# A fourth input slot, a bank reader moved to ScalarE, and a changed order on VectorE in a convolution kernel

## The chip, the cores and the metric

The kernel runs on one core of a Trainium2 chip. The metric is the device time of one execution in microseconds (us). The five engines of the core (TensorE or PE, VectorE or DVE, ScalarE or ACT, GpSimd or POOL, SyncE or SP) each run a program of their own in order and meet at semaphores. Transfers are issued on SyncE's queue and run on 16 DMA engines.

## The reference

The input x has 8 images of 64 channels and 224 x 224 pixels. It is group-normalised in 32 groups. The result is x plus two terms: a 3 x 3 convolution of the normalised x with its bias (`res`), and a map that comes from the first image alone (wavelet filters, an attention on each group of channels, another 3 x 3 convolution and a leaky ReLU) and is added to every image:

```python
x = x + _L0_conv_ref(_gn(x), ...)
# in _L0_conv_ref:
res = conv3x3(x, W_id, b_id)
cA, cH, cV, cD = _swt2_level3(x[0])
...
out = jax.nn.leaky_relu(conv3x3(dmt, W_enc, b_enc), 0.01)
return out + res
```

## The kernel before

The kernel has three stages: what comes before the maps, the maps of the first image (`encoder`), and the convolution of the eight images (`main`), which is the stage of the change. It begins near 800 us and fills the rest of the time. The map of the encoder stays in on-chip memory (`e_map`) and is added by seeding the PSUM banks with it.

**Bands.** The two halves of an image's rows lie on the lower and the upper 64 partitions. Each half has 14 bands of 8 rows, with two rows more for the neighbours, so a band is 128 x 2240 values of float32. Weights and data are split into a high and a low part in float16, and three products of the parts (high-high, low-high, high-low) are accumulated. Seven bands of an image are *direct*: three rows of weights for each output row, into `g_bank[0]` (PSUM banks 0 and 1) and `g_bank[1]` (banks 2 and 3). Seven are *minimal*: they form differences of rows (in place, rows 0 to 7 of the band) and sums of rows (`sums`), and need four products `m0` to `m3` in `a_bank` (banks 4, 5) and `b_bank` (banks 6, 7) instead of six.

**Rounds.** The stage has 56 rounds. In round q TensorE works on the direct band q+1 and the minimal band q, in turn: `first_direct` (72 matmuls), `product_m2` (36), `middle_direct` (72), `product_m1` (36), `last_direct` (72), `product_m0` (36), `product_m3` (36). All matmuls have line L1766, and a round has 360. `product_m1` overwrites what `double` reads, so it waits for `double`. `product_m0` waits for `seed_odd`.

**VectorE's round** is written out by hand: `odd_rows(q-1)` (L1969, two instructions, waits for `m3` of round q-1, which is the end of that round on TensorE), `diffs_low(q)` (L1946), `neighbour_sums(q+1)` (L1928, L1929), a part of the next image's weights in two of the seven rounds of an image (`build_part`, L1734 to L1745), `read_direct(q+1, 0)` (L1954), `split(q+2)` (L1619), `seed_odd(q)` (L1961), `differences(q+1)` (L1935), `sums_low(q+1)` (L1940), `read_direct(q+1, 1)` (L1954).

**ScalarE's round**: `diffs_high(q)` (L1863), `high(q+2)` (L1606), `double(q)` (L1879, writes `twice` = -2 times `a_bank` plus a mean), `full(q+2)` (L1612), `seed_direct(q+2, 0)` (L1633), `sums_high(q+1)` (L1871), `even_rows(q)` (L1886, waits for `m0`), `seed_minimal(q+1)` (L1893), `seed_direct(q+2, 1)` (L1633).

**Results.** `stage[0]` holds the results of a direct band and `stage[1]` those of a minimal band, each 128 x 1792; in `stage[1]` the left half of each group of 448 columns holds even rows and the right half odd rows. `stored[0]` and `stored[1]` count the stores that have landed, four of 224 KB for a band, 16 counts each.

**SyncE's round** q: wait for both readers of the direct band q, four stores (L1833); wait for the even and the odd rows of band q-1, four stores (L1833); two loads of x of two transfers each (L1584). A load into a slot waits until the band that lay there has been split into its parts (`split_done`).

**Memory.** There are XS = 3 slots for bands of x. The six sets of weights in float32 (`base`, three loaded, three made by GpSimd in `sets`) and `twice` lie behind the first two slots, `made` holds a half of the six sets while it is built.

Of the kernel before, what the change touches and what calls it, by code (L numbers as in the profile page):

```python
# [18 lines left out]
P = 128  # L19
# [8 lines left out]
RH = R + 2  # L28
NT = 2 * W
XS = 3  # L30
# [51 lines left out]
Ahead = namedtuple("Ahead", "load weights_load dummies pads norms spread build normed high full split edges root partners sets spread_rows clear first_seed conv_first conv_rest")  # L82
# [831 lines left out]
def encoder(nc, x, t, scratch, rows_last, rows_out, step_in, ps, psum, sb, sem, top, weff, u32, b32, bn, b16, shift, inside, e_max, einv, b_id, early, e_map,  # L914
# [5 lines left out]
    with ExitStack() as s4:  # L920
# [72 lines left out]
        def sync(sp):  # L993
# [45 lines left out]
            ahead.load(sp, 2)  # L1039

# [310 lines left out]
        def gpsimd(pool):  # L1351
# [89 lines left out]
            both_rows(NE - 1)  # L1441

# [3 lines left out]
def main(nc, x, t, out, ps, psum, sb, sem, top, pool_of, early, e_map, partner, mv_all, norm_all, w_max, unit):  # L1446
# [3 lines left out]
    with ExitStack() as s5:  # L1450
        tail = sb(s5, "tail", [P, RH * W + 4 * NT * 2 + V_N + SET_N + TMP_N])
# [23 lines left out]
        assert 2 * RH * W + SET_N + 4 * W <= D_EVEN_AT  # L1475
        x_hi = [f16_rows(pooled(AT_HI0, HI_N), RH), f16_rows(pooled(AT_HI0 + 2 * HI_N, HI_N), RH)]
        x_lo = [f16_rows(pooled(AT_HI0 + HI_N, HI_N), RH), f16_rows(early[:, RH * W:RH * W + HI_N], RH)]
        sums = pooled(AT_S, 2 * CH * W)
        first_made = sums[:, 0:TMP_N].rearrange("p (s k e) -> p s k e", s=NSET // 2, k=3)
# [3 lines left out]
        diag = early[0:C, RH * W:RH * W + B * C].rearrange("p (i e) -> p i e", i=B)  # L1483
# [5 lines left out]
        made = carve(TMP_N).rearrange("p (s k e) -> p s k e", s=NSET // 2, k=3)  # L1489
# [35 lines left out]
        g_read = sem(top, "g_read")  # L1525
# [18 lines left out]
        built = sem(top, "built")  # L1544
# [45 lines left out]
        def weights_load(sp):  # L1590
            for s in range(2):
                sp.dma_start(base[C * s:C * s + C, 0:3, :, :].rearrange("p s k e -> p (s k) e"), t["w_id"]).then_inc(weights_in, 16)
            sp.dma_start(ident, t["ident"]).then_inc(weights_in, 16)
# [34 lines left out]
        def seed_direct(act, j, g):  # L1628

            i, b = direct(j)  # L1630
            if j:
                act.wait_ge(g_read, 2 * j - 1 + g)
            act.activation(g_bank[g], e_rows[:, :, b, g, :, :].rearrange("p r q w -> p r (q w)"), ACT.Identity,  # L1633
                           scale=lane(r_out, i), bias=lane(mean_r, i)).then_inc(g_seeded, 1)
# [72 lines left out]
        def sets(pool):  # L1707
# [7 lines left out]
            def of(s):  # L1715
                return base[:, s, :, :].rearrange("p k e -> p (k e)")
# [8 lines left out]

        def build_part(dve, i, h):

            n = 10 * i + 1 + 5 * h
            v = made if i else first_made
            flat = v.rearrange("p s k e -> p (s k) e")  # L1730
            if i == 0 and h == 0:
                dve.wait_ge(sets_made, 6)
            dve.wait_ge(building, n)
            dve.tensor_tensor(flat, base[:, 3 * h:3 * h + 3, :, :].rearrange("p s k e -> p (s k) e"),  # L1734
# [93 lines left out]
        def sync(sp):  # L1828
# [16 lines left out]
            load(sp, 3)  # L1845
            load(sp, 4)
            for q in range(NW):
                store_direct(q)
                if q:
                    store_minimal(q - 1)  # L1850
                load(sp, 2 * q + 5)
                load(sp, 2 * q + 6)
# [4 lines left out]
        def scalar(act):  # L1857
# [39 lines left out]
            for q in range(-1, NW):  # L1897
# [14 lines left out]
                if q + 1 < NW:  # L1912
                    seed_minimal(q + 1)
                if q + 2 < ND:
                    seed_direct(act, q + 2, 1)

        def vector(dve):
            def neighbour_sums(j):

                i, b = minimal(j)  # L1920
                k = place_w(j)
                landed(dve, k)
# [26 lines left out]
            def read_direct(j, g):  # L1949
# [3 lines left out]
                dve.wait_ge(g_done, 2 * j + g + 1)  # L1953
                dve.tensor_scalar(stage[0][:, :, g, :], g_bank[g], lane(m_out, i), None, ALU.mult).then_inc(g_read, 1)  # L1954

            def seed_odd(j):
# [4 lines left out]
                dve.tensor_tensor(b_bank, a_bank, twice, ALU.add).then_inc(b_seeded, 1)  # L1961
# [11 lines left out]
            for q in range(-1, NW):  # L1973
                if q > 0:
                    odd_rows(q - 1)
                if q >= 0:
                    diffs_low(q)
                if q + 1 < NW:
                    neighbour_sums(q + 1)
                i, b = direct(q + 1) if q + 1 < ND else (B, 0)  # L1980
                if i + 1 < B and b in DIRECT[2:4]:
                    build_part(dve, i + 1, DIRECT.index(b) - 2)
                if q + 1 < ND:
                    read_direct(q + 1, 0)
# [7 lines left out]
                if q + 1 < ND:  # L1992
                    read_direct(q + 1, 1)
# [17 lines left out]
        def gpsimd(pool):  # L2011
# [14 lines left out]
            for i in range(B):  # L2026
                if i + 1 < B:
# [5 lines left out]
                      sets=sets, spread_rows=spread_rows, clear=clear, first_seed=first_seed, conv_first=conv_first, conv_rest=conv_rest)  # L2033
# [43 lines left out]
```

## Time and profile before

| | |
|---|---|
| runs of the kernel | 1819.07 us median of 3 (1810.22 to 1823.49) |
| the profiled execution | 1814.87 us, of which the span of its instructions is 1813.1 us |
| granted TensorE clock, mean of the span | 0.994 |
| TensorE matmuls busy | 1761.4 us (97%) |
| VectorE busy | 1450.2 us (80%) |
| ScalarE busy | 1238.6 us (68%) |
| GpSimd busy | 545.5 us (30%) |
| stores of results | 448 of 224 KB, median 3.6 us from issue to landing |

Busy times are shares of the whole span, so they average over the three stages. Matmuls overlap one another, and a busy TensorE need not be at its peak rate; the number of matmuls that start in a stretch tells its rate. The granted clock is 1.00 at the upper of the two levels of TensorE's clock (2.4 GHz) and 0.50 at the lower (1.2 GHz).

### The profile page before, as it was taken

To read this page: it belongs to the slowest core of one execution; us is meant where nothing else is said; L and a number is where in the kernel's file an instruction comes from. 1 tells how busy PE (TensorE), PEld (TensorE's weight loads), DVE (VectorE), ACT (ScalarE), POOL (GpSimd) and SP (SyncE) were. 2 spreads that over 40 slices of the span, in tenths; PEclk is the share of its full clock that TensorE was granted. 3 is DMA by queue.
4 is the path that set the end of the run, shared out by engine and by line. 5 is a ranking of instruction groups with operands and counts; after the bars stand their busy time and mean duration, and the time that the engine had idled before them with its cause. 6 is when DMAs were issued, how large, how long until landed. Compare 5 with 4: busy or idle time off the path is not lost. (4 is left out here: it accounts for less than half of the span.)

```text
span 1813.1 us, 69228 instructions
## 1 busy us (share of the span) xinstructions
PE 1761.4 (97%) x31540; PEld 1470.2 (81%) x31540; DVE 1450.2 (80%) x1926; ACT 1238.6 (68%) x1339; POOL 545.5 (30%) x365
## 2 busy tenths in 40 slices
PE   9999999999999999989999999999999999999997
PEld 9997999999999999965577797767966756967676
DVE  5665578778777887668989889888889888888886
ACT  5555666666666666667776777767776767766774
POOL 0005788888888888640000000000000000000000
PEclk9999999999999999999999999999999999999999
DMA  8884399888888888458998998998989989989994
GB/s 186 245 296 126 122 274 227 212 219 216 212 215 215 215 215 206 100 125 204 235 234 223 239 239 226 240 240 229 238 224 236 247 213 232 242 219 230 249 234 140
DMA packets 132964, 391.84 MB, mean 216 GB/s; under 512 B 49884, under 2 KB 50656, under 8 KB 118464
## 3 DMA queue, kind: packets, MB, share of 16 engines
q1 hardware_dynamic: 132672, 387.43, 82.7%
q8 instruction: 247, 4.05, 1.0%
q14 instruction: 45, 0.37, 0.1%
HBM read 258.88 MB, written 128.45 MB: 214 GB/s over the span
## 5 line engine op out<-in xcount | busy, mean ns | idle before, releaser
L1766 PE MATMUL ps<-big,tail 64*64 64x448 f16 x3840 | 323.3, 353 | 11.8 <-DVE ps L1961 7.8
L1766 PE MATMUL ps<-pool_of 64*64 64x448 f16 x5184 | 302.5, 352 | 7.9 <-DVE pool_of L1625 4.2
L1766 PE MATMUL ps<-pool_of,tail 64*64 64x448 f16 x4896 | 300.1, 349 | 0.7 <-issue 0.7
L1766 PE MATMUL ps<-big,pool_of 64*64 64x448 f16 x3552 | 278.5, 352 | 17.1 <-DVE ps L1961 11.9
L1292 DVE BATCH_NORM_STATS2 pool_of<-big 128x6 f32<-128x448 f32 x392 | 232.2, 616 | 76.4 <-DMA big<-in_x 76.3
L1766 PEld LDWEIGHTS ps<-pool_of 64*64 64x64 f16 x5184 | 196.2, 107 | 68.0 <-issue 10.1
L1766 PEld LDWEIGHTS ps<-pool_of,tail 64*64 64x64 f16 x4896 | 189.6, 106 | 59.3 <-issue 1.3
L1066 PE MATMUL ps<-pool_of 112*128 112x246 f16 x1344 | 218.8, 271 | 1.7 <-DVE pool_of L1280 0.8
L1070 PE MATMUL ps<-pool_of 112*128 112x168 f16 x1344 | 217.8, 243 | 0.0
L1766 PEld LDWEIGHTS ps<-big,tail 64*64 64x64 f16 x3840 | 169.0, 107 | 57.9 <-DVE ps L1961 10.4
L1069 PE MATMUL ps<-pool_of 112*128 112x90 f16 x1344 | 201.3, 206 | 0.0
L1766 PEld LDWEIGHTS ps<-big,pool_of 64*64 64x64 f16 x3552 | 134.3, 107 | 69.8 <-DVE ps L1961 15.8
L1886 ACT ACTIVATE tail<-ps,pool_of 128x896 f32<-128x896 f32 x56 | 56.5, 1008 | 180.8 <-PE ps L1766 180.8
L2019 POOL MEMSET pool_of<- 64x224 f32 x5 | 1.4, 277 | 558.5 <-DVE tail L1946 558.5
L1633 ACT ACTIVATE ps<-big,pool_of 128x896 f32<-128x896 f32 x112 | 122.5, 1095 | 55.0 <-DVE tail L1954 52.5
L1766 PE MATMUL ps<-tail 64*64 64x448 f16 x1344 | 155.5, 353 | 0.6 <-issue 0.6
L1100 PE MATMUL ps<-d_odd,shared 128*64 128x224 f16 x3024 | 148.1, 259 | 0.3 <-DVE pool_of L1280 0.3
L1100 PE MATMUL ps<-pool_of,shared 128*64 128x224 f16 x3024 | 148.3, 259 | 0.0
L628 PE MATMUL ps<-fh,pool_of 112*112 112x238 f32 (+1 forms) x512 | 144.3, 364 | 2.5 <-DVE big L860 1.3
L1100 PEld LDWEIGHTS ps<-d_odd,shared 128*64 128x64 f16 x3024 | 143.8, 110 | 2.6 <-issue 0.8
L1100 PEld LDWEIGHTS ps<-pool_of,shared 128*64 128x64 f16 x3024 | 143.8, 110 | 1.7 <-issue 0.2
L1766 PE MATMUL ps<-tail,pool_of 64*64 64x448 f16 x1344 | 143.5, 352 | 0.3 <-issue 0.3
(252 smaller groups left out, 3809.8 us busy)
## 6 DMA issues: line engine op xcount, KB each, us to landing
out<-tail SPq DMA_DIRECT2D x448, 224.0 KB, 3.6
big<-in_x SPq DMA_DIRECT2D x392, 224.0 KB, 5.2
pool_of<-in_x SPq DMA_DIRECT2D x139, 560.0 KB, 7.4
tail<-in_x SPq DMA_DIRECT2D x69, 560.0 KB, 7.4
pool_of<-row_filtered SPq DMA_DIRECT2D x110, 224.0 KB, 4.0
row_filtered<-big SPq DMA_DIRECT2D x2, 6272.0 KB, 22.8
pool_of<-in_x SPq DMA_DIRECT2D x30, 392.0 KB, 7.1
row_filtered<-big SPq DMA_DIRECT2D x4, 1568.0 KB, 9.2
```

Of the source, the lines that this page charges most:

```text
L628: pe.matmul(o[:, 0:width], xg[g][:, near, c % CG, :], fh[:, near, first:first + width], start=True, stop=False)
L1066: pe.matmul(tiles(o)[:, :, 15:NTILE], lhs[:, 1, a, :], tiles(v)[:, :, 15:NTILE], start=(k == 0), stop=False)
L1069: pe.matmul(tiles(o)[:, :, 0:15], lhs[:, 0, a, :], tiles(v)[:, :, 0:15], start=False, stop=False)
L1070: mm = pe.matmul(both(o), lhs[:, 0, a, :], both(v), start=False, stop=(k == 2))
L1100: mm = pe.matmul(o[s], weff[a][:, sw, i, ky, :], d[n][:, b, r:r + 4, sw, NTILE * i:NTILE * i + NTILE], start=(k == 0), stop=(k == len(piec ...
L1292: ins = dve.bn_stats(records[:, 2 * (k % CHN) + i, :], sx[k % 4][:, i * NT:i * NT + NT])
L1633: act.activation(g_bank[g], e_rows[:, :, b, g, :, :].rearrange("p r q w -> p r (q w)"), ACT.Identity, scale=lane(r_out, i), bias=lane(mean ...
L1766: mm = pe.matmul(psum[bank + r][C * k:C * k + C, 0:NT], wt[i % 2][lanes, h, s, kx, :], v[u][lanes, rows_of(k), kx:kx + W], start=False, st ...
L1886: act.activation(stage[1][:, :, :, 0:W], a_bank.rearrange("p r (g w) -> p r g w", g=2), ACT.Identity, scale=lane(m_out, i)).then_inc(even_ ...
L2019: pool.memset(xs[k % XS][up, 0:W], 0.0).then_inc(filled, 1)
```

## The change

Four things change, all for the last stage.

- The slots for x become four (XS = 4). The fourth lies behind the first two, where `base` and `twice` were. The second half of the six weight sets is made there first (`early_base`) and copied to its place (`base[1]`, in the memory that `made` had) by GpSimd in `keep`; the load of the fourth slot waits for this copy, for the first image's weights and for the end of the map.
- `twice` lies in the right halves of `stage[1]`. `double` waits for the stores of the minimal band before, and the odd rows, which go to the same place, wait for `seed_odd`, the last reader of `twice`.
- ScalarE reads the second bank of a direct band (`read_second`), after the seed of the next minimal band. Each bank has its own semaphore `g_read`.
- On VectorE, the weight part and then `neighbour_sums(q+1)` come before `diffs_low(q)`.

```diff
-XS = 3
+XS = 4
...
@@ encoder, sync
             sp.wait_ge(conv_done, 2 * NE)
             ahead.load(sp, 2)
+            ahead.first_kept(sp)
+            sp.wait_ge(map_done, NE)
+            ahead.load(sp, 3)
@@ encoder, gpsimd
             both_rows(NE - 1)
+            pool.wait_ge(conv_done, 2 * NE)
+            ahead.keep(pool)
@@ main
-        xs = [pooled(0, RH * W), pooled(RH * W, RH * W), carve(RH * W)]
-        base = pooled(2 * RH * W, SET_N).rearrange("p (s k e) -> p s k e", s=NSET, k=3)
-        twice = pooled(2 * RH * W + SET_N, 4 * W).rearrange("p (r n) -> p r n", r=2)
+        xs = [pooled(0, RH * W), pooled(RH * W, RH * W), carve(RH * W), pooled(2 * RH * W, RH * W)]
...
+        twice = stage[1][:, :, :, W:NT]
...
+        def keep(pool):
+            pool.tensor_copy(base[1].rearrange("p s k e -> p (s k e)"), early_base.rearrange("p s k e -> p (s k e)")).then_inc(kept, 1)
+
+        def first_kept(sp):
+            sp.wait_ge(kept, 1)
+            sp.wait_ge(building, 11)
@@ main, sync
             def store_direct(j):
-                sp.wait_ge(g_read, 2 * j + 2)
+                for g in range(2):
+                    sp.wait_ge(g_read[g], j + 1)
                 store(*direct(j), 0)
@@ main, scalar, double
                 if j:
                     act.wait_ge(b_seeded, j)
-                act.activation(twice, a_bank, ACT.Identity, scale=-2.0, bias=lane(mean_r2, i)).then_inc(twice_ready, 1)
+                    act.wait_ge(stored[1], 64 * j)
+                act.activation(twice, a_bank.rearrange("p r (g w) -> p r g w", g=2), ACT.Identity, scale=-2.0, bias=lane(mean_r2, i)).then_inc(twice_ready, 1)
...
+            def read_second(j):
+                i, b = direct(j)
+                if j:
+                    act.wait_ge(stored[0], 64 * j)
+                act.wait_ge(g_done, 2 * j + 2)
+                act.activation(stage[0][:, :, 1, :], g_bank[1], ACT.Identity, scale=lane(m_out, i)).then_inc(g_read[1], 1)
...
                 if q + 1 < NW:
                     seed_minimal(q + 1)
+                if q + 1 < ND:
+                    read_second(q + 1)
                 if q + 2 < ND:
                     seed_direct(act, q + 2, 1)
@@ main, vector
             def odd_rows(j):
                 i, b = minimal(j)
                 dve.wait_ge(odd_done, j + 1)
-                if j:
-                    dve.wait_ge(stored[1], 64 * j)
+                dve.wait_ge(b_seeded, j + 1)
...
-                if q >= 0:
-                    diffs_low(q)
-                if q + 1 < NW:
-                    neighbour_sums(q + 1)
                 i, b = direct(q + 1) if q + 1 < ND else (B, 0)
                 if i + 1 < B and b in DIRECT[2:4]:
+                    dve.wait_ge(sums_split, q + 1)
                     build_part(dve, i + 1, DIRECT.index(b) - 2)
+                if q + 1 < NW:
+                    neighbour_sums(q + 1)
+                if q >= 0:
+                    diffs_low(q)
                 if q + 1 < ND:
-                    read_direct(q + 1, 0)
+                    read_first(q + 1)
...
-                if q + 1 < ND:
-                    read_direct(q + 1, 1)
             odd_rows(NW - 1)
```

## Rows read from the trace of the kernel before

**Rows 1.** Windows: length; PE, PEld, DVE, ACT, POOL busy; clock, DMA share, GB/s.

```profile
1010.00:1060.00 50.00, 50.00 (x1058) 42.92 (x1052) 43.53 (x34) 37.61 (x27) 0.65 (x2) 1.00 0.93 237
```

**Rows 2.** Timeline of VectorE: odd rows that open the second and the last round.

```profile
833.41 1.27 DVE L1969 SCALAR_TENSOR_TENSOR tail<-ps,pool_of,big 128x448 f32<-128x448 f32 x2
...
1795.91 1.27 DVE L1969 SCALAR_TENSOR_TENSOR tail<-ps,pool_of,big 128x448 f32<-128x448 f32 x2 [0.77 <-PE ps L1766]
```

**Rows 3.** What TensorE waited for at L1766, in all: us, times.

```profile
  DVE ps L1961: 19.7, 15
```

**Rows 4.** Timeline of TensorE: start, us, instructions [idle before, releaser].

```profile
796.00 9.94 PE L1766 MATMUL ps<-pool_of 64*64 64x448 f16 x144 [4.17 <-DVE pool_of L1625]
...
822.82 0.57 PE L1766 MATMUL ps<-big,pool_of 64*64 64x448 f16 x8 [1.63 <-ACT pool_of L1879]
...
992.38 0.57 PE L1766 MATMUL ps<-big,tail 64*64 64x448 f16 x8 [1.94 <-DVE ps L1961]
...
1117.10 0.57 PE L1766 MATMUL ps<-big,pool_of 64*64 64x448 f16 x8 [1.96 <-DVE ps L1961]
```

**Rows 5.** Windows of 8 us behind three gaps.

```profile
796.00:804.00 8.00, 8.00 (x108) 4.67 (x112) 3.99 (x5) 6.16 (x9) 2.56 (x4) 0.63 0.93 201
...
992.00:1000.00 8.00, 7.62 (x128) 4.31 (x132) 6.58 (x6) 4.63 (x4) 0.00 (x0) 0.79 0.86 191
1117.00:1125.00 8.00, 7.90 (x166) 5.09 (x170) 6.30 (x7) 5.05 (x5) 0.00 (x0) 1.00 0.87 203
```

**Rows 6.** Timeline of ScalarE in a round: even rows, seed, `double`, `full`.

```profile
1030.37 1.01 ACT L1886 ACTIVATE tail<-ps,pool_of 128x896 f32<-128x896 f32 x1 [3.28 <-PE ps L1766]
1031.41 1.10 ACT L1893 ACTIVATE ps<-big,pool_of 128x896 f32<-128x896 f32 x1
...
1037.31 0.99 ACT L1879 ACTIVATE pool_of<-ps,pool_of 128x896 f32<-128x896 f32 x1
1038.20 2.24 ACT L1612 ACTIVATE pool_of<-pool_of,norm_all 128x2240 f32<-128x2240 f32 x1
```

**Rows 7.** Timeline of VectorE: `split`, `seed_odd`, `diffs_low`.

```profile
1023.37 2.50 DVE L1619 TENSOR_TENSOR big<-pool_of 128x2240 f16<-128x2240 f32 x1
1025.77 1.09 DVE L1961 TENSOR_TENSOR ps<-ps,pool_of 128x896 f32<-128x896 f32 x1
...
1035.29 2.09 DVE L1946 SCALAR_TENSOR_TENSOR tail<-tail,norm_all,big 128x1792 f16<-128x1792 f32 x1 [1.93 <-ACT big L1863]
```

**Rows 8.** Timeline of SyncE's queue: eight stores of one round, twice.

```profile
1031.88 5.74 SPq L1833 DMA_DIRECT2D out<-tail  x8
...
1206.44 6.59 SPq L1833 DMA_DIRECT2D out<-tail  x8
```

**Rows 9.** The last store of each of these: duration, start; us from issue to landing.

```profile
L1833 SPq DMA_DIRECT2D out<-tail x1: 796/796/796, 1036.8 to 1036.8; - x1
...
DMA to landing us min/median/max: 3.9/3.9/3.9
...
L1833 SPq DMA_DIRECT2D out<-tail x1: 1055/1055/1055, 1212.0 to 1212.0; - x1
...
DMA to landing us min/median/max: 4.5/4.5/4.5
```

**Rows 10.** All stores: issue in ns min/median/max; landing.

```profile
L1833 SPq DMA_DIRECT2D out<-tail x448: 466/599/1839, 816.9 to 1809.4; - x150
...
DMA to landing us min/median/max: 2.8/3.6/6.0
```

**Rows 11.** Timelines of GpSimd, TensorE and VectorE: start and end of the stage.

```profile
809.75 1.13 POOL L1392 TENSOR_TENSOR big<-big 128x448 f32<-128x448 f32 x1 [2.00 <-ACT big L1166]
...
1796.48 0.57 PE L1766 MATMUL ps<-big,tail 64*64 64x448 f16 x8 [0.61 <-ACT ps L1893]
...
1806.29 1.27 DVE L1969 SCALAR_TENSOR_TENSOR tail<-ps,pool_of,big 128x448 f32<-128x448 f32 x2 [3.74 <-PE ps L1766]
```

**Rows 12.** The page, DMA issues: transfers, KB each, median us to landing.

```profile
pool_of<-in_x SPq DMA_DIRECT2D x139, 560.0 KB, 7.4
```

More of the change, by code:

```diff
@@ L81 @@
 Link = namedtuple("Link", "cleared einv_ready b32_in act_rows dve_rows first_split emx emax_part emax_all spread_max sx stat_in unit")
-Ahead = namedtuple("Ahead", "load weights_load dummies pads norms spread build normed high full split edges root partners sets spread_rows clear first_seed conv_first conv_rest")
+Ahead = namedtuple("Ahead", "load weights_load dummies pads norms spread build normed high full split edges root partners sets keep first_kept spread_rows clear first_seed conv_first conv_rest")
 def input_transform():
@@ L1471, in main @@
         assert AT_S + 2 * CH * W <= SMALL_AT - NREC * 6
[L1472 to L1475 removed]
+        xs = [pooled(0, RH * W), pooled(RH * W, RH * W), carve(RH * W), pooled(2 * RH * W, RH * W)]
+        assert 3 * RH * W <= D_EVEN_AT
         x_hi = [f16_rows(pooled(AT_HI0, HI_N), RH), f16_rows(pooled(AT_HI0 + 2 * HI_N, HI_N), RH)]
[L1477 removed]
+        x_lo = [f16_rows(pooled(AT_HI0 + HI_N, HI_N), RH), f16_rows(early[:, V_N:V_N + HI_N], RH)]
         sums = pooled(AT_S, 2 * CH * W)
[L1479 removed]
+        made = sums[:, 0:TMP_N].rearrange("p (s k e) -> p s k e", s=NSET // 2, k=3)
         lanes_of = pooled(SMALL_AT - NREC * 6, C + 10 * B)
@@ L1488, in main @@
         wt = [weights_of(pooled(AT_W0, SET_N)), weights_of(carve(SET_N))]
-        made = carve(TMP_N).rearrange("p (s k e) -> p s k e", s=NSET // 2, k=3)
+        base = [v.rearrange("p (s k e) -> p s k e", s=NSET // 2, k=3) for v in (early[:, V_N + HI_N:V_N + HI_N + TMP_N], carve(TMP_N))]
+        early_base = xs[3][:, 0:TMP_N].rearrange("p (s k e) -> p s k e", s=NSET // 2, k=3)
+        twice = stage[1][:, :, :, W:NT]
         e_rows = e_map[:, 0:NE * EN].rearrange("p (r b g q w) -> p r b g q w", r=2, b=NB, g=2, q=2)
@@ L1524, in main @@
         g_done = sem(top, "g_done")
-        g_read = sem(top, "g_read")
+        g_read = [sem(top, f"g_read{g}") for g in range(2)]
         a_seeded = sem(top, "a_seeded")
@@ L1543, in main @@
         building = sem(top, "building")
-        built = sem(top, "built")
+        kept = sem(top, "kept")
         TOP, BOTTOM = 0, NB - 1
@@ L1732, in build_part @@
                 dve.wait_ge(sets_made, 6)
+            if i == 1 and h == 1:
+                dve.wait_ge(kept, 1)
             dve.wait_ge(building, n)
-            dve.tensor_tensor(flat, base[:, 3 * h:3 * h + 3, :, :].rearrange("p s k e -> p (s k) e"),
+            dve.tensor_tensor(flat, (base[h] if i or h == 0 else early_base).rearrange("p s k e -> p (s k) e"),
                               r_rows[:, i, :].unsqueeze(1).broadcast_to((P, 9, C)), ALU.mult).then_inc(building, 1)
@@ L1843, in store_minimal @@
                 store(*minimal(j), 1)
-            load(sp, 3)
-            load(sp, 4)
+            load(sp, XS)
+            load(sp, XS + 1)
             for q in range(NW):
@@ L1850, in sync @@
                     store_minimal(q - 1)
-                load(sp, 2 * q + 5)
-                load(sp, 2 * q + 6)
+                load(sp, 2 * q + XS + 2)
+                load(sp, 2 * q + XS + 3)
             store_minimal(NW - 1)
@@ L1921, in neighbour_sums @@
                 k = place_w(j)
+                if j:
+                    dve.wait_ge(sums_split, j)
                 landed(dve, k)
@@ L1952, in read_direct @@
                     dve.wait_ge(stored[0], 64 * j)
-                dve.wait_ge(g_done, 2 * j + g + 1)
-                dve.tensor_scalar(stage[0][:, :, g, :], g_bank[g], lane(m_out, i), None, ALU.mult).then_inc(g_read, 1)
+                dve.wait_ge(g_done, 2 * j + 1)
+                dve.tensor_scalar(stage[0][:, :, 0, :], g_bank[0], lane(m_out, i), None, ALU.mult).then_inc(g_read[0], 1)
             def seed_odd(j):
@@ L1960, in seed_odd @@
                     dve.wait_ge(odd_read, 2 * j)
-                dve.tensor_tensor(b_bank, a_bank, twice, ALU.add).then_inc(b_seeded, 1)
+                dve.tensor_tensor(b_bank.rearrange("p r (g w) -> p r g w", g=2), a_bank.rearrange("p r (g w) -> p r g w", g=2), twice, ALU.add).then_inc(b_seeded, 1)
             def odd_rows(j):
@@ L1975, in vector @@
                     odd_rows(q - 1)
+                i, b = direct(q + 1) if q + 1 < ND else (B, 0)
+                if i + 1 < B and b in DIRECT[2:4]:
+                    dve.wait_ge(sums_split, q + 1)
+                    build_part(dve, i + 1, DIRECT.index(b) - 2)
+                if q + 1 < NW:
+                    neighbour_sums(q + 1)
                 if q >= 0:
                     diffs_low(q)
-                if q + 1 < NW:
-                    neighbour_sums(q + 1)
-                i, b = direct(q + 1) if q + 1 < ND else (B, 0)
-                if i + 1 < B and b in DIRECT[2:4]:
-                    build_part(dve, i + 1, DIRECT.index(b) - 2)
                 if q + 1 < ND:
-                    read_direct(q + 1, 0)
+                    read_first(q + 1)
                 if q >= 0 and q + 2 < ND:
```

16 lines of the change are left out of this document (8 added, 8 removed).

## Prediction

> **What bounds the kernel now.** I read the last stage alone, from about 812 us on, since the change works there. First the windows of the stage: in a stretch without weight building TensorE is busy for the whole 50.00 us and starts 1058 matmuls, 47.3 ns apart [rows 1]. A round has 360 of them, so TensorE alone needs 17.0 us a round. Then VectorE's first instruction of a round, which waits for the end of the round before: from the second round to the last lie 54 rounds in 962.5 us, 17.82 us each [rows 2]. What a perfect change could win is therefore 0.8 us a round, 44 us in all. Next, what TensorE waits for: 19.7 us in 15 waits go to `seed_odd`, L1961 [rows 3]; the gaps come in pairs, one pair for each image, where VectorE builds the next image's weights, and the longer gap of a pair is 1.94 to 1.97 us in six images, of which two are shown [rows 4]. After some of them the clock drops to its lower level for a while: the mean over the next 8 us is 0.79 after the gap that ends at 992.38 us, which is 1.7 us lost, and 1.00 after the one at 1117.10 [rows 5]; of the six, three dropped. A gap of 4.17 us at the start of the stage was followed by 0.63, 3.0 us lost [rows 4, 5].
>
> **The readers and the reordering.** ScalarE takes the reading of the second bank, about 1.0 us by the row of the same size that it already reads from PSUM (L1886) [rows 6]; VectorE loses as much or a little more. `diffs_low` now stands behind the sums, which cover the 1.93 us that it waited for ScalarE [rows 7]. Together VectorE gains about 3 us a round, more than a part of the weights takes, so the waits on `seed_odd` and the clock drops behind them would go: 19.7 + 3 x 1.7 = 25 us at most. The fourth slot lets each load start a whole slot earlier; no row of before shows a wait for x inside the stage, so it is worth nothing there, and it costs nothing.
>
> **The wait that is added.** `twice` moves into the right halves of `stage[1]`. These are what the odd rows are stored from, so `double(q)` now waits until the store of band q-1 has landed. Behind `double` in ScalarE's queue stand `full`, the next seed, the sums' high part and the even rows; TensorE waits for `double` itself before `product_m1`. That such a delay reaches TensorE at once the trace shows in the very first round, where `double` came late and TensorE stood for 1.63 us [rows 4].
>
> When does that store land? SyncE issues the four stores of the direct band q, then the four of the minimal band q-1. Both wait their turn in one queue, and the first four wait for the second bank's reader, which the change puts on ScalarE behind the even rows and the next seed. So one round closes on itself, and its length is the sum of this loop:
>
> - From the first store's issue to the landing of the eighth. At 1031.88 us eight issues begin; the last begins at 1036.8 and lands 3.9 us later, 8.8 us in all. At 1206.44 us: last issue at 1212.0, landing 4.5, so 10.1 [rows 8, 9]. I take 9.4, the middle of the two.
> - `double` to the start of `full` 0.89, `full` 2.24 [rows 6]; `split`, to the start of `seed_odd`, 2.40; `seed_odd` 1.09 [rows 7].
> - `product_m0`, which needs `seed_odd`: 36 x 47.3 ns = 1.70.
> - Even rows 1.04 to the next start, the next band's seed the same (1.10 less the overlap), then the second bank's reader 1.0 [rows 6]. Then the stores are issued again.
>
> The sum is 9.4 + 0.89 + 2.24 + 2.40 + 1.09 + 1.70 + 1.04 + 1.04 + 1.0 = 20.8 us, against 17.8: **3.0 us a round, 54 x 3.0 = 163 us**. TensorE's own branch, from `double` over 0.99 + 108 matmuls (5.1), is 0.5 us shorter than the 6.6 us of `full`, `split` and `seed_odd`. Counted from the start of a round (even rows start 1.7 us before it), the stores begin at 1.4, the last lands at 10.8, `double` ends at 11.8, while TensorE is ready for `product_m1` after 180 matmuls, at 8.5: it stands 3.3 us in every round. The weight parts now fit into VectorE's wait for `split`, so nothing of them is left to pay; their saving is contained in the 17.8 that the loop replaces.
>
> The Trainium skill (DMA: Bandwidth & Descriptors, Anatomy of one DMA) gives a transfer, on GpSimd's path, 2.0 us plus its bytes at 436 GB/s, an estimate of 2.5 us for 224 KB; the loop would be 1.7 us shorter than with the 4.2 us of the two rows, and the total some 92 us lower. The trace disagrees: eight stores of one queue follow each other here.
>
> **The clock.** A gap of 3.3 us lies between 1.95 us (three drops in six) and 4.17 us (one in one); between these rows I take four rounds in five to drop, an estimate. One drop loses 1.7 us [rows 5], of which the 0.5 us that TensorE would have waited before `product_m0` is covered: 1.2 x 0.8 x 54 = 52 us. Bounds: 0, and 135 us if every gap is followed by the loss of 3.0.
>
> The Trainium skill (TensorE: Matmul & The Clock Gate, HAM oscillation) tells of a kernel whose clock falls back at every wait for a transfer, tile after tile. By that every round would drop, 65 us instead of 52; the rows for the shorter gap do not show it.
>
> **Start and end of the stage.** The fourth load now waits for GpSimd's copy, which follows the last map addition at 809.75 + 1.13 us [rows 11]; the same engine took 1.13 us for 448 columns, so about 1.5 for 576, and the load is issued near 812.4. With 7.4 us to landing [rows 12] it is there at 819.8; `high`, which reads that band and stands ahead of the `double` of 822 us [rows 4], hardly moves, but the band after it is needed by the sums, and `diffs_low` now stands behind these. I take 2 us, bounds 0 and 6. In the last round there is no direct band to fill TensorE: it took from 1796.48 us to the last odd rows at 1806.29, 9.8 us, without any of this wait [rows 11]. With the landing at 10.8, `double` to 11.8, `product_m1` and `seed_odd` to 14.6 and two products it takes 18.0: 8 us more.
>
> **Sum.** The profiled execution took 1814.87 us (span 1813.1, 1.8 around it; the median of the three runs is 1819.07, 0.2% above): 1814.9 + 163 + 52 + 2 + 8 = **2040 us**.
>
> **Rivals.**
> - *The stores are through sooner.* The round is longer, so fewer loads lie beside the stores. With seven issues at the median 0.6 us and the median landing of 3.6 us [rows 10] the first term is 7.8, the loop 19.2, the gap 1.7 us; with a drop in half the rounds (0.6 us) the sum is 1815 + 54 x (1.4 + 0.6) + 10 = 1933. Against it: the loads ahead of the stores are issued behind `split`, as now, and eight stores of 224 KB at the 237 GB/s of the stage [rows 1] need 7.7 us by themselves.
> - *Every gap drops the clock, and longer.* With 2.5 us net in each round (loss of 3.0 less 0.5): 2040 - 52 + 135 = 2123. For it: the gap is nearer to 4.17 than to 1.95 us.
> - *The landing is hidden; faster.* If the eighth store landed within 6.1 us of the first issue, `double` would end at 1.4 + 6.1 + 1.0 = 8.5 us, when TensorE gets there, and VectorE's relief would stand: 1815 - 25 + 2 = 1792. That is the point from which it decides. Seven issues at the shortest, 0.47 us, and the shortest landing, 2.8 [rows 10], just make it; the two groups of eight shown took 8.8 and 10.1, and their issues alone 5.74 and 6.59 [rows 8].
>
> **Chances.** Forecast 0.60; stores through sooner 0.17; every gap with the longer loss 0.17; landing hidden, faster 0.04; hidden, but the gain lost at the start of the stage, no change 0.02. The range runs from 1925 (below the quicker stores) to 2115 (most of the longer clock loss) and leaves out the hidden landing and the top of the last case. A change of about 1% is the least that a measurement of this kernel tells from none: faster by over 1% 0.04, within 1% 0.02, slower 0.94.
>
> **What the profile after would show.** ScalarE's `double` waits for the store, some 5 us in each of about 55 rounds, where before it waited at most for TensorE. TensorE's largest wait is for `double`, about 3 us each; a second, about 0.5 us, for `seed_odd` in the rounds without a drop; the pairs of waits for each image are gone. A round is 20.8 us without a drop of the clock and 22 with one; windows of 8 us behind the gap show 0.79 in most rounds. SyncE waits for ScalarE's reader before the direct stores. DMA engines are busy for some 75% instead of 93%, ScalarE and VectorE idle more. The prediction fails if the eighth store lands in under 7 us from the first issue, or if the store of the direct band starts earlier than 1 us into the round.

## The result, and the profile after

The changed kernel takes 2080.49 us (median of 4 runs, 2074.67 to 2087.62) against 1817.56 us for the kernel before, measured beside it (1810.22 to 1823.49). The ratio is 1.1451, with a 95% interval from 1.1395 to 1.1507. The profiled execution of after took 2074.67 us, with a span of 2072.9 and a mean clock of 0.957 (before 0.994); it is 259.8 us longer than the profiled execution of before.

First VectorE's timeline, which says where these 259.8 us lie. The rows are the odd rows that open the second, the last and no further round, as in [rows 2, 11].

```profile
846.94 1.27 DVE L1996 SCALAR_TENSOR_TENSOR tail<-ps,pool_of,big 128x448 f32<-128x448 f32 x2 [2.22 <-PE ps L1781]
...
2046.44 1.28 DVE L1996 SCALAR_TENSOR_TENSOR tail<-ps,pool_of,big 128x448 f32<-128x448 f32 x2 [2.88 <-PE ps L1781]
...
2066.10 1.28 DVE L1996 SCALAR_TENSOR_TENSOR tail<-ps,pool_of,big 128x448 f32<-128x448 f32 x2 [3.74 <-PE ps L1781]
```

- Start of the stage: 846.94 - 833.41 = 13.5 us later.
- The 54 rounds: 2046.44 - 846.94 = 1199.5 us, 22.21 each, against 962.5: 237.0 us more.
- The end: from the last round's opening to the end of the span 26.5 us against 17.2, 9.3 us more.

Next the waits between 846 and 2046 us, the 54 rounds. Each line names who waited and for whom; the numbers are us in all, times, and the longest.

```profile
ACT tail L1896 <- DMA out<-tail: 248.5, 54, 7.0
PE ps L1781 <- ACT tail L1896: 182.9, 54, 4.8
DVE tail L1982 <- DMA out<-tail: 41.9, 34, 2.6
PE ps L1781 <- DVE ps L1989: 6.3, 14, 0.8
```

Read the first two together. `double` (L1896 now) waits for a store in every round, 4.6 us on average, and TensorE waits for `double` in every round, 3.4 us. The fourth line is what stands in the place of [rows 3]: the waits for `seed_odd` (L1989) are short ones, 0.45 us, in 14 rounds.

The chain itself, on three engines. SyncE's queue (start, duration, number of issues), and behind it the last store of the second group with its landing, as in [rows 8, 9]:

```profile
1204.77 5.69 SPq L1848 DMA_DIRECT2D out<-tail  x8
...
1226.55 5.80 SPq L1848 DMA_DIRECT2D out<-tail  x8
```

```profile
L1848 SPq DMA_DIRECT2D out<-tail x1: 942/942/942, 1231.4 to 1231.4; - x1
...
DMA to landing us min/median/max: 3.9/3.9/3.9
```

ScalarE's timeline, the counterpart of [rows 6]:

```profile
1203.69 0.99 ACT L1911 ACTIVATE tail<-ps,pool_of 128x896 f32<-128x896 f32 x1
...
1213.79 1.01 ACT L1896 ACTIVATE tail<-ps,pool_of 128x896 f32<-128x896 f32 x1 [4.10 <-DMA out<-tail]
1214.70 2.24 ACT L1617 ACTIVATE pool_of<-pool_of,norm_all 128x2240 f32<-128x2240 f32 x1
...
1223.41 1.01 ACT L1903 ACTIVATE tail<-ps,pool_of 128x896 f32<-128x896 f32 x1 [3.28 <-PE ps L1781]
...
1235.40 1.01 ACT L1896 ACTIVATE tail<-ps,pool_of 128x896 f32<-128x896 f32 x1 [3.93 <-DMA out<-tail]
...
1244.17 1.01 ACT L1903 ACTIVATE tail<-ps,pool_of 128x896 f32<-128x896 f32 x1 [2.92 <-PE ps L1781]
```

And TensorE's, the counterpart of [rows 4]:

```profile
1214.85 0.59 PE L1781 MATMUL ps<-big,pool_of 64*64 64x448 f16 x4 [2.66 <-ACT tail L1896]
...
1236.46 0.57 PE L1781 MATMUL ps<-big,pool_of 64*64 64x448 f16 x8 [2.86 <-ACT tail L1896]
...
1242.20 0.57 PE L1781 MATMUL ps<-big,pool_of 64*64 64x448 f16 x8 [0.42 <-DVE ps L1989]
```

The second bank's reader (L1911) ends at 1204.68 and the stores are issued from 1204.77. In the next round the eighth store is issued at 1231.4 and lands 3.9 us later, at 1235.3; `double` starts at 1235.40, TensorE at 1236.46. The loop of the forecast is there, step behind step, and it closes in every round: over the 54 rounds the means of its three parts, 9.49 us from the first store to `double`, 9.60 from `double` to the even rows and 3.14 from there to the next first store, add up to 22.23.

The clock, by windows (length; busy time of PE, PEld, DVE, ACT, POOL; clock, DMA share, GB/s): the 54 rounds, and 8 us behind two of the gaps, as in [rows 5].

```profile
845.00:2047.00 1202.00, 1010.11 (x19472) 587.29 (x19465) 785.39 (x617) 746.93 (x540) 4.89 (x15) 0.94 0.71 183
...
1214.00:1222.00 8.00, 7.15 (x120) 3.86 (x124) 4.96 (x3) 5.73 (x4) 0.28 (x1) 0.79 0.61 148
1236.00:1244.00 8.00, 7.12 (x148) 4.17 (x152) 5.35 (x4) 5.25 (x4) 0.00 (x0) 1.00 0.57 135
```

A round with the drop and one without it stand here beside each other. The DMA engines are busy for 71% of the rounds, and TensorE for 84%.

### The profile page after: what moved, and what is told of

It reads as the page before. It is cut to its first block, busy times and chain, and to the rows that moved or that the text cites. A ratio compares the mean times of both kernels' runs of the same rounds, so it can differ in the third digit from the quotient of the medians.

```text
span 2072.9 us, 69348 instructions
## 1 busy us (share of the span) xinstructions
PE 1837.8 (89%) x31540; PEld 1356.9 (65%) x31540; DVE 1395.6 (67%) x1870; ACT 1292.1 (62%) x1395; POOL 547.6 (26%) x366
## 4 chain that ended last, share of the span: by engine, by line
PE 19%; SPq 13%; DMA 12%; ACT 10%; issue 6%; DVE 1%; POOL 0%; ACTq 0%; DVEq 0%
PE ps L1781 19%; SPq L1848 13%; DMA out<-tail 12%; ACT tail L1896 3%; ACT tail L1903 3%; ACT tail L1911 3%; ACT pool_of L1617 2%; DVE ps L1989 1%; DVE pool_of L1624 0%; SPq L1589 0%; DVE big L1624 0%; ACT big L1169 0%; POOL tail L1733 0%; ACTq L1895 0%; POOL big L1399 0%
## 5 line engine op out<-in xcount | busy, mean ns | idle before, releaser
L1781 PE MATMUL ps<-big,tail 64*64 64x448 f16 x3840 | 311.7, 378 | 104.6 <-ACT tail L1896 101.5
L1781 PE MATMUL ps<-big,pool_of 64*64 64x448 f16 x3552 | 282.4, 375 | 104.1 <-ACT tail L1896 90.3
L1781 PEld LDWEIGHTS ps<-big,tail 64*64 64x64 f16 x3840 | 116.7, 113 | 194.9 <-ACT tail L1896 113.5
L1781 PEld LDWEIGHTS ps<-big,pool_of 64*64 64x64 f16 x3552 | 106.2, 112 | 192.0 <-ACT tail L1896 102.4
L1781 PEld LDWEIGHTS ps<-pool_of 64*64 64x64 f16 x5184 | 157.1, 110 | 114.1 <-issue 18.1
L1896 ACT ACTIVATE tail<-ps,pool_of 128x896 f32<-128x896 f32 x56 | 56.4, 1007 | 255.7 <-DMA out<-tail 255.7
L1781 PEld LDWEIGHTS ps<-pool_of,tail 64*64 64x64 f16 x4896 | 150.5, 111 | 98.1 <-issue 15.5
L1903 ACT ACTIVATE tail<-ps,pool_of 128x896 f32<-128x896 f32 x56 | 56.4, 1007 | 200.2 <-PE ps L1781 200.2
L1624 DVE TENSOR_TENSOR big<-pool_of 128x2240 f16<-128x2240 f32 x28 | 69.9, 2495 | 146.2 <-ACT pool_of L1617 146.2
L1624 DVE TENSOR_TENSOR pool_of<-pool_of 128x2240 f16<-128x2240 f32 x28 | 69.9, 2495 | 140.2 <-ACT pool_of L1617 140.0
```

Of the source, the lines that this page charges most:

```text
L1624: ins = dve.tensor_tensor(x_lo[p][:, :, 1:1 + W], xs[place_d(j) % XS].rearrange("p (r w) -> p r w", w=W), x_hi[p][:, :, 1:1 + W], ALU.subt ...
L1781: mm = pe.matmul(psum[bank + r][C * k:C * k + C, 0:NT], wt[i % 2][lanes, h, s, kx, :], v[u][lanes, rows_of(k), kx:kx + W], start=False, st ...
L1896: act.activation(twice, a_bank.rearrange("p r (g w) -> p r g w", g=2), ACT.Identity, scale=-2.0, bias=lane(mean_r2, i)).then_inc(twice_rea ...
```

## The experiments

Ten kernels were run, each against the kernel before on the same chip. "Round" is the time from the second to the last opening of a round, divided by 54; it is 17.82 us before and 22.21 after.

**The wait alone** (e2): the kernel before, with nothing but `twice` moved.

```diff
-        twice = pooled(2 * RH * W + SET_N, 4 * W).rearrange("p (r n) -> p r n", r=2)
+        twice = stage[1][:, :, :, W:NT]
...
                     act.wait_ge(b_seeded, j)
+                    act.wait_ge(stored[1], 64 * j)
```

> The kernel before with one change: the doubled product lies in the right halves of the second stage, with the wait for the store. Readers, order and slots are as before. Theory: almost the whole loss comes back, since the loop closes through VectorE instead of ScalarE. From the first of eight stores to the double 9.5, double to seed_odd's start 5.7, then seed_odd 1.0, differences 1.9, lower sums 2.0 and the second bank's reader 1.15: 21.2 us a round. The drop of the clock lies beside this loop and not in it. 1815 + 54 x 3.4 + 9 = about 2008 us, 2060 if the clock counts here too. Rival (the reader's place on ScalarE makes the loss, the store alone would be in time): 1815 to 1850 us.

Measured: 2026.19 us, ratio 1.1145 [1.1119, 1.1171], a round of 21.63 us. Its waits between 840 and 2000 us (here `double` is L1880):

```profile
ACT tail L1880 <- DMA out<-tail: 255.5, 54, 7.3
PE ps L1766 <- ACT tail L1880: 155.5, 54, 4.5
```

So this one wait makes 209 of the 263 us by itself, with VectorE still reading both banks and three slots of x; the expectation of 2008 to 2060 us holds. The profiled executions of e2 and of the changed kernel are 47 us apart: 31 in the rounds, 12 at the start of the stage and 3 at its end.

**All but the wait** (e1): three slots and `twice` in its own memory as before, but ScalarE reads the second bank and `diffs_low` follows the sums.

```diff
+            def read_second(j):
...
+                act.activation(stage[0][:, :, 1, :], g_bank[1], ACT.Identity, scale=lane(m_out, i)).then_inc(g_read[1], 1)
...
-                if q >= 0:
-                    diffs_low(q)
                 if q + 1 < NW:
                     neighbour_sums(q + 1)
+                if q >= 0:
+                    diffs_low(q)
...
-                    read_direct(q + 1, 1)
```

> The kernel before with the second bank read by ScalarE and the sums ahead of the differences' lower halves; three slots, and the doubled product in memory of its own, so that nothing waits for a store. Theory (the wait for the store of the minimal band makes the whole loss): the loss is gone, VectorE's relief stands, the pairs of waits on seed_odd for each image go; 1785 to 1805 us against 1817. Rival one (the reader on ScalarE, with the work behind it, makes ScalarE the bound): above 1900 us. Rival two (the order needs the fourth slot: the sums wait for x in every round): some 1.2 us or more a round, 1880 us or more, with VectorE's wait for a load in its rows.

Measured: 1816.77 us, ratio 0.9995 [0.9981, 1.0009], a round of 17.86 us. The loss is gone, but the gain that I expected is not there, and none of the three forecasts holds. The sign of rival two is in the rows of VectorE between 850 and 1780 us: the sums, which now come earlier, wait for x.

```profile
DVE pool_of L1940 <- DMA pool_of<-in_x: 77.4, 29, 4.4
DVE pool_of L1940 <- DMA tail<-in_x: 39.0, 13, 4.4
```

With the fourth slot (e10, e11) no such wait is listed. In e1 it does not reach TensorE through `seed_odd`, as TensorE's waits in the same stretch show, first of before, then of e1 (`seed_odd` is L1961 and L1973):

```profile
PE ps L1766 <- DVE ps L1961: 17.2, 12, 2.0
PE ps L1766 <- issue: 8.7, 12, 1.1
```

```profile
PE ps L1766 <- issue: 26.8, 22, 2.4
PE ps L1766 <- DVE ps L1973: 1.5, 4, 0.6
```

The waits for `seed_odd` went, 15.7 us of 17.2, and as much came back in gaps for which the profile shows no releaser ("issue"), 18.1 us. What TensorE stood for, the trace's DMA packets tell.

Queue q8, which the page of the profile calls "instruction", moves packets of 16 KB. There are 247 of them in before, after and e1; in e4 and e9, where TensorE has 6,912 and 13,824 more instructions (matmuls and weight loads), there are 274 and 301. So these are TensorE's instructions, 256 to a packet. Each of the 22 gaps of e1 ends 1.25 to 1.65 us after the end of such a packet, and so do those of before, e10 and e11 (1.21 to 1.61); none of TensorE's gaps with a releaser in these four runs does. TensorE waited for its instructions.

One of the longest gaps of e1 stands in the middle of a product of 72 matmuls. From 1002.6 to 1014.0 us no packet of q8 starts, where the median between two is 5.6 us; the second line is of the 1.4 us behind that.

```profile
1016.63 0.90 PE L1766 MATMUL ps<-pool_of,tail 64*64 64x448 f16 x5 [2.41 <-issue]
```

```profile
q8 instruction: 1, 0.02, 6.1%
```

Why a packet comes late is not shown.

**The reader without the reordering** (e8): e1 with the old order of `diffs_low` and the sums.

> The kernel before with the second bank's reader on ScalarE and nothing else changed (order, slots and doubled product as before). Theory: diffs_high stands behind the reader on ScalarE, so diffs_low, for which VectorE already waits 1.9 us a round, comes 1.0 us later; ordinary rounds have 1.7 us to spare, the rounds with weights have not: 1825 to 1850 us against 1817. Rival (VectorE loses 1.14 us of work and so the waits on seed_odd shrink): 1800 to 1810 us.

Measured: 1834.13 us, ratio 1.0082 [1.0064, 1.0099], a round of 18.10 us. The waits between 850 and 1780 us show `diffs_low` (L1958) waiting longer for ScalarE (90.3 us before), which the reader has made later, and TensorE behind `seed_odd`:

```profile
DVE tail L1958 <- ACT big L1864: 143.7, 51, 3.0
...
PE ps L1766 <- DVE ps L1973: 23.5, 13, 2.1
```

The two edits belong together: without the reordering, the reader loses 0.8%. Of the 15 us, 6.3 are longer waits for `seed_odd`, and 6.4 more gaps without a releaser (15.1 us against 8.7).

**The minimal band's stores first** (e3): the changed kernel, with the two calls exchanged.

```diff
-                store_direct(q)
                 if q:
                     store_minimal(q - 1)
+                store_direct(q)
```

> The changed kernel with the four stores of the minimal band issued ahead of those of the direct band. Theory: four issues instead of eight stand before the awaited landing, so the double starts some 7.1 us into the round and no longer holds TensorE; the direct stores land as late as the minimal ones did, and the reader of the first bank, which waits for them, is next: split and seed_odd move behind it and a round is about 19.1 us; with the start and the end of the stage 1900 us, up to 1945 with drops of the clock. Rival (the transfers as a whole are the bound, not the order of their issue): no change from 2075 to 2088 us.

Measured: 1934.9 us, ratio 1.0653 [1.0629, 1.0676], a round of 19.60 us. Its waits between 850 and 1900 us:

```profile
DVE tail L1982 <- DMA out<-tail: 232.4, 54, 6.3
ACT tail L1896 <- DMA out<-tail: 79.3, 54, 2.9
PE ps L1781 <- DVE ps L1989: 80.6, 53, 3.0
```

`double`'s wait fell from 248.5 to 79.3 us, and the first bank's reader (L1982), whose stores are now last, took over with 232.4. It is the place in the queue of eight that sets which wait is long.

**The reader ahead of the even rows** (e5): the changed kernel, with the direct stores' reader earlier in ScalarE's queue.

```diff
+                if q + 1 < ND:
+                    read_second(q + 1)
                 if q >= 0:
                     even_rows(q)
                 if q + 1 < NW:
                     seed_minimal(q + 1)
-                if q + 1 < ND:
-                    read_second(q + 1)
```

> The changed kernel with one reordering on ScalarE: the second bank's reader stands ahead of the even rows and the next seed, so it runs as soon as TensorE has finished the direct band. Theory (the round is set by when the eight stores can start and by the four that stand ahead of the awaited ones): the direct stores start some 2.4 us before the round instead of 1.4 us into it, the minimal ones behind the odd rows at 1.3, the last lands near 7.1 and the double ends at 8.1, before TensorE is ready at 8.5. The loop is open, a round is 17.2 to 17.9 us, and what is left against before is the start of the stage (13.5) and its last round (5): 1800 to 1840 us. Rival (any wait for a store's landing in the double costs about what it cost, whatever is issued ahead of it): above 1980 us.

Measured: 1900.47 us, ratio 1.0447 [1.043, 1.0465], a round of 19.00 us. 180 us came back, but 60 to 100 us less than expected. The timelines of SyncE and of VectorE in one round:

```profile
1306.99 9.99 SPq L1589 DMA_DIRECT2D pool_of<-in_x  x4
1317.69 6.81 SPq L1848 DMA_DIRECT2D out<-tail  x8
```

```profile
1320.69 1.27 DVE L1996 SCALAR_TENSOR_TENSOR tail<-ps,pool_of,big 128x448 f32<-128x448 f32 x2
```

Behind them in this round, the last store with its landing, and `double`:

```profile
L1848 SPq DMA_DIRECT2D out<-tail x1: 686/686/686, 1323.8 to 1323.8; - x1
...
DMA to landing us min/median/max: 5.3/5.3/5.3
```

```profile
1329.24 1.01 ACT L1896 ACTIVATE tail<-ps,pool_of 128x896 f32<-128x896 f32 x1 [3.34 <-DMA out<-tail]
```

The stores begin 3.0 us before the odd rows now, but the last of them still store those odd rows: the eighth is issued at 1323.8 and takes 5.3 us to land, at 1329.1. `double` follows at once. Over the 54 rounds the eighth store takes 4.80 us to land (4.28 in the changed kernel), and the first follows the last load's issue after 1.7 us (6.8); that the loads make the difference is not shown. The loop now runs through the odd rows in place of the direct band's reader, which the expectation had not reckoned with.

**Filling the gap** (e4, e9): the changed kernel, with 64 matmuls whose sums nobody reads ahead of TensorE's wait for `double`, to keep the clock up; e9 has them in fp32.

```diff
+            if j and j + 1 < ND:
+                for n in range(64):
...
+                    pe.matmul(psum[2 + n % 2][...], wt[minimal(j)[0] % 2][lanes, 0, 4, 0, :], v_hi[lanes, 12, 1:65], start=False, ...)
             pe.wait_ge(twice_ready, j + 1)
```

> The changed kernel with 64 small matmuls (64 columns each, into columns of PSUM that nothing reads) between the middle product and the wait for the double, in the rounds 1 to 54: TensorE works through most of the gap. They add work that the result doesn't use. Theory (the gap is followed by a lower clock that costs about 1 us a round in the loop): the granted clock of the stage rises from 0.94 to above 0.98, a round falls from 22.2 to about 21.4 us, 2030 to 2045 us. Rival (the lower clock is hidden behind full, split and seed_odd, or is no consequence of the gap): 2070 to 2090 us.

> The changed kernel with 64 float32 matmuls of 64 columns between the middle product and the wait for the double, into columns that nothing reads; the small float16 ones of the run before filled 0.7 us of a gap of 3.4, these should fill 2 to 3 us. They add work that the result doesn't use. Theory (the drop of the clock after the gap costs about 1 us a round): granted clock of the stage above 0.98, a round near 21.4 us, 2030 to 2045 us. Rival (the loop through the store alone sets the round): 2065 to 2085 us.

Measured: e4 2070.86 us, ratio 1.1392 [1.1359, 1.1424]; e9 2103.59 to 2146.39 us, ratio 1.1607 [1.1553, 1.166]. Neither reaches the theory's 2030 to 2045 us. In e4, by TensorE's timeline, the 64 matmuls filled 0.69 us of the gap and left 3.16:

```profile
1230.29 0.69 PE L1818 MATMUL ps<-big,pool_of 64*64 64x64 f16 x64
...
1234.14 0.57 PE L1781 MATMUL ps<-big,pool_of 64*64 64x448 f16 x8 [3.16 <-ACT tail L1901]
```

Still the clock fell in fewer rounds of e4, 28 of 54 against 40, and its mean over the rounds is 0.96 instead of 0.94:

```profile
847.00:2032.00 1185.00, 1021.67 (x22908) 625.66 (x22896) 784.14 (x617) 744.24 (x538) 4.90 (x15) 0.96 0.73 186
```

Its rounds are 21.93 us, 15 us less in all, or 1.3 us for each of the 12 drops that went. The medians of the runs lie 10 us apart and their ranges touch (2062 to 2078 against 2075 to 2088 us), so this supports a price of about 1 us for a drop and does not settle it.

In e9 the waits between 850 and 2080 us show that the wait for `double` shrank from 3.4 us to 1.3 (in 49 rounds), while the matmuls behind the added ones stood in gaps without a releaser. These too end 1.24 to 1.62 us after a packet of q8, all 57 of them (74.4 us before the kernel's own matmuls, 22.5 before the added ones): e9 made TensorE wait for its instructions.

```profile
PE ps L1781 <- issue: 74.4, 45, 4.3
PE ps L1781 <- ACT tail L1901: 62.9, 49, 3.3
```

**The start** (e7): e5, with GpSimd's copy moved ahead of its `inner(NE - 1)`, and the fourth load waiting for an earlier step than the map's end.

```diff
+            pool.wait_ge(conv_done, 2 * NE)
+            ahead.keep(pool)
             inner(NE - 1)
...
-            pool.wait_ge(conv_done, 2 * NE)
-            ahead.keep(pool)
...
             ahead.first_kept(sp)
-            sp.wait_ge(map_done, NE)
+            sp.wait_ge(z_part, NE)
```

> As the run with the early reader, and GpSimd's copy of the weight sets is issued as soon as the encoder's last products are done, ahead of the last map work, with the fourth load waiting for the part of the map that uses its memory instead of the map's end. Theory (13.5 us of the loss come from this copy and the loads behind it): 8 to 11 us less than the run with the early reader alone; 1792 to 1830 us. Rival (the start is late for another reason, the loads' own time): within 3 us of that run.

Measured: 1885.66 us, ratio 1.0368 [1.035, 1.0386]. The second round opens at 833.20 us, against 844.89 in e5, and the medians are 14.8 us apart, where 8 to 11 were expected. The delay of the start thus comes from the copy's place and the load's wait; which of the two gives how much was not taken apart. It is not the copy's own time: in e5 the copy took 0.66 us, and the second round still opens 11.5 us later than before.

```profile
813.16 0.66 POOL L1733 COPY tail<-pool_of 128x576 f32<-128x576 f32 x1
```

**`twice` in memory of its own** (e10, e11): the changed kernel, with `twice` as float16 in free memory and without the store's wait; e11 has e7's start as well.

```diff
-        twice = stage[1][:, :, :, W:NT]
+        twice = pool_of.bitcast(F16)[...]
...
                     act.wait_ge(b_seeded, j)
-                    act.wait_ge(stored[1], 64 * j)
...
-                dve.wait_ge(b_seeded, j + 1)
+                if j:
+                    dve.wait_ge(stored[1], 64 * j)
```

> The changed kernel whole, with four slots, ScalarE's reader and the new order, but the doubled product in free memory of its own, as float16 instead of float32 since no more is free, so that the double waits for no store; the odd rows wait for it as they did before. The rounding of the doubled product changes. Theory (the wait behind the shared memory is the whole loss in the rounds): a round falls from 22.2 us to 17.1 to 17.9, the double waits for no transfer, and what is left against before is the start of the stage, 10 to 14 us: 1795 to 1835 us. Rival (the rounds stay long by the reader, the order or the load on the queue): above 1900 us.

> As the run with the doubled product in its own memory, and the copy of the weight sets moved to the encoder's last products with the fourth load waiting for less. Theory one (VectorE's relief and the fourth slot are worth something once nothing waits for a store): rounds of 17.1 to 17.5 us and no late start, 1780 to 1805 us against 1818. Theory two (what the three-slot kernel without the wait showed: relief is eaten by TensorE's waits for no event of the profile and by the transfers, which fill the DMA engines to 0.90): 1808 to 1825 us, with such waits of TensorE near 27 us as there.

Measured: e10 1814.52 us, ratio 0.9982 [0.9971, 0.9994], a round of 17.62 us. e11 1804.59 us, ratio 0.9929 [0.991, 0.9947], a round of 17.68 us: 0.7% faster than the kernel before and 13% faster than the changed one. TensorE's waits in e11, 850 to 1780 us:

```profile
PE ps L1784 <- issue: 21.8, 21, 2.6
PE ps L1784 <- DVE ps L1991: 0.4, 1, 0.4
```

The waits for `seed_odd` are gone for good (0.4 us, before 17.2), and the gaps in which TensorE waits for its instructions have taken most of their place (21.8 us, before 8.7), as in e1. So e10 is as it was expected. The time of e11 lies just inside theory one (1780 to 1805 us), but its rounds do not (17.1 to 17.5 us); theory two had the gaps right in kind, and their length too high (27 us).

## Why the prediction was right, and where its terms were off

The forecast of 2040 us was for the profiled execution, which took 2074.67: 35 us more, of which 22 lie in the rounds, 11.5 at the start of the stage and 1.3 at its end. All three terms came out too small, so the total owes nothing to errors that cancel. The measured median lies midway between the forecast and the rival in which every gap drops the clock (2123 us); the rows below, not the time, tell the two apart.

**The cause is shown.** The wait of `double` for the store makes the loss: alone it costs 209 us (e2), and without it the rest of the change is within 0.2% of before (e1, e10). In e10 this is a sum of two: 10.6 us lost at the start and 11.1 won in the rounds. That the loop passes through SyncE's queue of eight is shown by e3 and e5, which only exchange its parts and give back 146 and 180 us.

**The rounds, 163 + 52 = 215 us forecast, 237 measured.** The terms of the loop, as means over the 54 rounds:
- First store to `double`: 9.4 forecast; 9.49 measured (8.53 to 10.79).
- `double` to the even rows: 8.32 forecast without a drop of the clock, 8.80 measured in the 14 rounds without one. The 0.48 are the steps between engines and the last matmuls' end, which the sum left out; in 54 rounds they make 26 us, the larger part of what is missing. In the round of 1235.40 us TensorE goes on for `seed_odd` at 1242.20, after 6.80 us where 6.62 were summed; the even rows (L1903) of that round start at 1244.17, 1.97 us later where I had 36 x 47.3 ns = 1.70.
- Even rows to the first store: 3.08 forecast, 3.14 measured.
- The clock: in 40 of the 54 rounds the granted clock fell behind the gap. These are the rounds without a second gap, for `seed_odd`, and in them `double` to the even rows takes 9.88 us, 1.08 more; the two windows above are one of each kind. 40 x 1.08 = 43 us, forecast 52 (1.2 us in four of five). Whole rounds of the two kinds, from `double` to `double`, differ by less, 22.39 against 21.76, since behind a round without a drop the next first store to `double` took longer, 9.83 us against 9.38; why is open. By whole rounds the clock is worth 40 x 0.63 = 25 us. e4 supports the term, with 15 us for 12 drops, but no experiment separates it; its size is argued from rows. The rival's 2.5 us net in every round is not there.

The Trainium skill (DMA: Bandwidth & Descriptors, Anatomy of one DMA) gave the estimate of 2.5 us for one store, and a total 92 us lower. Its figure is for one transfer on GpSimd's path; it does not carry over to these stores, eight in a row from SyncE, of which the last took 4.28 us to land over the 54 rounds (3.13 to 6.00).

The Trainium skill (TensorE: Matmul & The Clock Gate, HAM oscillation) would have every round drop. The trace does not agree: three in four did, midway between that and the three in six that the rows of the shorter gap gave.

**The start, 2 us forecast, 13.5 measured: the term that failed.** Two things were off in it, as the timelines of GpSimd, SyncE, VectorE and TensorE show.

```profile
812.14 2.55 POOL L1733 COPY tail<-pool_of 128x576 f32<-128x576 f32 x1
```

```profile
814.71 3.66 SPq L1589 DMA_DIRECT2D pool_of<-in_x  x6
```

```profile
829.11 1.15 DVE L1956 SCALAR_TENSOR_TENSOR pool_of<-pool_of 128x896 f32<-128x896 f32 x1 [11.83 <-DMA pool_of<-in_x]
```

```profile
815.10 0.96 PE L1781 MATMUL ps<-pool_of 64*64 64x448 f16 x8 [4.36 <-POOL tail L2040]
...
840.86 0.96 PE L1781 MATMUL ps<-big,pool_of 64*64 64x448 f16 x8 [8.33 <-DVE ps L1989]
```

The copy took 2.55 us, not 1.5, and GpSimd's clearing of the padding, which stands behind it in the queue, kept TensorE 4.36 us. The larger part is the queue of SyncE: it waits at the fourth load, so the fifth and sixth, which I had left where they were, went out with it at 814.71. Before, the fourth and fifth were both issued by 804.0 us:

```profile
795.92 8.12 SPq L1584 DMA_DIRECT2D pool_of<-in_x  x4
```

The sums of the second band waited 11.83 us for theirs, the fifth, and `seed_odd` stands behind them on VectorE. I had bounded this at 6 us from the one load, not from the loads behind it. e5 and e10 tell the two apart: with a copy of 0.66 us their second rounds still open 11.5 and 10.6 us late. e7 gives 11.7 us back.

**The fourth slot** was worth nothing inside the stage in the forecast, and its cost is the start. The reordered sums do wait for x with three slots, 116 us in e1, a wait that no row of before had, and with four they don't; what this is worth in time was not taken apart.

**The end, 8 us forecast, 9.3 measured.** TensorE waited 8.84 us for `double` in the last round:

```profile
2057.74 0.96 PE L1781 MATMUL ps<-big,tail 64*64 64x448 f16 x8 [8.84 <-ACT tail L1896]
```

**VectorE's relief, 25 us at most forecast for the case without the wait.** Without the store's wait the 54 rounds changed by +2 us in e1, -11 in e10 and -8 in e11 (17.86, 17.62 and 17.68 us each against 17.82), with the waits for `seed_odd` all but gone in the three. So the rival of 1792 us would have missed as well: by the relief, of which TensorE's waits for its instructions take back half or more (8.5 us of 17.0 in e10, 13.1 of 16.8 in e11, 18.1 of 15.7 in e1), and by the start, where e10 loses 10.6 us (second round at 844.01). The forecast had no term for these waits: it took all that `seed_odd` held back as time that TensorE would gain.

## What to carry to other kernels

Memory that is free "by then" costs a wait on whatever made it busy: where that is a transfer, follow the wait back through its landing, its queue and its reader, since these can close a loop that is longer than the round (here 22.2 us against 17.8). When a queue gets a new wait, list every transfer behind it. And before a helper engine is relieved, see what the bound engine waits for when that helper is never late (here its own instructions).

## What the runs showed of the hardware

- TensorE can stand for its own instructions. They arrive on q8 in packets of 16 KB, 256 instructions each, and all of TensorE's gaps without a shown releaser in before, e1, e10 and e11 (70 between 850 and 1780 us) end 1.2 to 1.65 us after the end of such a packet. They make 8.7 us before, 26.8 in e1, 17.2 in e10 and 21.8 in e11; in e9, with 64 fp32 matmuls a round more, the 57 gaps make 96.9 us between 850 and 2080 us. Why a packet comes late stays open.
- GpSimd's copy of 128x576 fp32 took 2.46 to 2.55 us in after, e3 and e4, and 0.66 us in e5, e7, e9, e10 and e11. VectorE's `differences` of 128x1792 ran beside it in six of the eight, and either the copy was long or `differences`: it took 2.01 to 2.20 us beside the long copies and 2.49 to 2.51 beside the short ones of e5, e9 and e10.
- The eighth store of a group landed after 4.28 us on average in after (3.13 to 6.00) and 4.80 in e5 (3.19 to 5.83), where the loads are issued closer ahead of the group. Within after the landing does not follow that distance, so the cause is open.
